# A feed-forward stage with block-scaled integers: normalization, copies and biases moved between the engines of one core, and its tile loop skewed

## The reference

```python
def _L2_ffn_ref(inputs, ln_w, ln_b, W1, b1, W2, b2):      # inputs = layernorm(x)
    bf16_round = lambda x: x.astype(bfloat16).astype(float32)
    def mx_quant(x):          # blocks of 32 along the last axis share one exponent
        s = x.shape
        xb = x.reshape(s[:-1] + (s[-1] // 32, 32))
        amax = max(abs(xb), axis=-1)
        scale = exp2(floor(log2(amax)) - 6)
        return clip(round(xb / scale), -128, 127) * scale
    def mx_linear(x, W, b):
        return bf16_round(mx_quant(x) @ mx_quant(W).T + b)
    x = residual = bf16_round(inputs)
    h = bf16_round(layernorm(x) * ln_w + ln_b)            # 256 wide
    h = mx_linear(h, W1, b1)                              # 1024 wide
    h = bf16_round(gelu_tanh(h))
    h = mx_linear(h, W2, b2)                              # 256 wide
    return bf16_round(residual + h)
...
x = x + tanh(g_ffn[2]) * _L2_ffn_ref(layernorm(x), ...)
```

## Time and profile before

| | |
|---|---|
| median of three runs | 966.0 us (963.3, 966.0, 970.25) |
| the profiled execution | 954.89 us, its span 953.1 us |
| TensorE busy over the span | 625.7 us, 66% |
| VectorE, ScalarE, GpSimd busy | 693.3, 318.1, 155.0 us |
| mean granted TensorE clock | 0.814 of full speed |
| stage 5 | 713.79 to 813.30 us of the span |

### The profile page before, as it was taken

One profiled execution on the slowest core, in us unless ns is written; L12 is line 12 of the kernel. 1 busy time (PEld: TensorE's weight loads), 2 busy tenths in 40 slices (PEclk: granted clock), 3 DMA queues, 4 the chain that ended last, 5 costly groups with the idle time before them and its releaser, 6 DMA issues. The chain is left out here.

```text
span 953.1 us, 9406 instructions
## 1 busy us (share of the span) xinstructions
PE 625.7 (66%) x2822; PEld 398.8 (42%) x2825; DVE 693.3 (73%) x1419; ACT 318.1 (33%) x543; POOL 155.0 (16%) x158
## 2 busy tenths in 40 slices
PE   5408998999973432389928488988970454339970
PEld 3303554555543431256817355555450222326540
DVE  5996699979969573597586759798859887843433
ACT  4004436545412321123234164655620322313210
POOL 0000001211200000344242001100114122014315
PEclk9759999999987655599968689999995565559995
DMA  8400002553558023134420032433527100013314
GB/s 238 101 13 0 7 0 45 88 89 66 89 127 244 0 61 136 39 108 125 101 61 17 1 88 53 96 77 86 133 45 175 46 1 1 22 37 94 93 60 128
DMA packets 57952, 71.17 MB, mean 75 GB/s; under 512 B 14920, under 2 KB 41424, under 8 KB 56752
## 3 DMA queue, kind: packets, MB, share of 16 engines
q1 hardware_dynamic: 45072, 42.53, 15.6%
q0 software_dynamic: 12832, 28.06, 14.9%
HBM read 43.43 MB, written 10.35 MB: 56 GB/s over the span
## 5 line engine op out<-in xcount | busy, mean ns | idle before, releaser
L521 PE MATMUL ps<-hT,regA 128*128 128x512 f32 x256 | 115.3, 593 | 1.3 <-ACT hT L437 1.3
L1855 PE MATMUL ps<-regA,regD 128*34 128x256 f32 x256 | 69.6, 395 | 16.3 <-DVE h L1973 10.8
L521 PEld LDWEIGHTS ps<-hT,regA 128*128 128x128 f32 x256 | 48.4, 190 | 52.1 <-issue 46.5
L532 PE MATMUL ps<-regA,regC 128*128 128x256 f32 x256 | 62.7, 388 | 6.8 <-DVE regC L651 5.3
L692 POOL DMA_DIRECT2D yssm<-regB x19 | 22.9, 1204 | 245.5 <-DVE regB L644 240.6
L532 PEld LDWEIGHTS ps<-regA,regC 128*128 128x128 f32 x256 | 46.7, 190 | 31.6 <-DVE regC L651 21.2
L447 ACT ACTIVATE regC<-ps 128x512 f32<-128x512 f32 x32 | 19.1, 597 | 91.1 <-PE ps L521 86.4
L1711 ACT ACTIVATE regA<-ps 128x512 f32<-128x512 f32 x64 | 38.1, 596 | 30.8 <-PE ps L1841 29.9
L636 DVE TENSOR_TENSOR_SCAN regB<-regB 128x512 f32<-128x512 f32 x38 | 44.5, 1212 | 2.8
L1242 POOL DMA_INDIRECT regA<-h_rows,regA x31 | 29.5, 952 | 73.6 <-DVE regA L1490 43.1
L1953 DVE TENSOR_REDUCE regC<-ps 128x4 f32<-128x960 f32 x64 | 39.7, 683 | 1.6 <-PE ps L1808 1.6
(11 more groups left out here) (400 smaller groups left out, 1524.9 us busy)
## 6 DMA issues: line engine op xcount, KB each, us to landing
yssm<-regB POOLq DMA_DIRECT2D x19, 512.0 KB, 5.0
regC<-bc_rows SPq DMA_DIRECT2D x26, 256.0 KB, 3.8
yssm<-regC POOLq DMA_DIRECT2D x13, 512.0 KB, 6.9
regB<-in_L_w SPq DMA_DIRECT2D x4, 1088.0 KB, 11.7
y_rows<-regA SPq DMA_DIRECT2D x31, 128.0 KB, 2.4
y_rows<-regB SPq DMA_DIRECT2D x23, 128.0 KB, 1.7
regB<-in_L_w SPq DMA_DIRECT2D x1, 2176.0 KB, 12.9
regC<-in_L_W SPq DMA_DIRECT2D x2, 1024.0 KB, 10.5
```

The costliest lines, as they stand in the source:

```text
L521: m = nc.tensor.matmul(ps[:, 2 + 2 * (u % 2) + j, :], w[:, k * 2048 + c * P:k * 2048 + (c + 1) * P], hT[:, k, hf * HALF:(hf + 1) * HALF], ...
L532: m = nc.tensor.matmul(ps[:, t // 2, (t % 2) * D:(t % 2 + 1) * D], itm[:, u % 2, t * P:(t + 1) * P], WDv[:, c // 2, c % 2, :], start=(c == ...
L1855: m = nc.tensor.matmul(ps[0:VW, 6 + j % 2, (n % 2) * S:(n % 2 + 1) * S], vaug[:, 2 * b + kt, hd, :], prob[:, n % 4, kt * S:(kt + 1) * S], ...
```

## The change

All of it is in stage 5.

- ScalarE does both normalizations, tile by tile, as `activation(Identity, scale=, bias=)`; VectorE computes scale and bias with one small operation more, and takes the statistics of `rb` tile by tile.
- The two bias rows are no more added by VectorE. They are loaded into partitions 0, 32 and 64 (`BROWS`) of `brows`, whose first 96 partitions (`NB5`) GpSimd clears before; ScalarE and GpSimd split them into three bfloat16 parts (`bcut`, `bsplit`), and TensorE adds them with one matmul more (`ones` times `bsplit`) in each bank of `up` and in the down product.
- The affine work (lnw, lnb) of pairs 0 and 2 goes to VectorE, that of pairs 1 and 3 stays on GpSimd.
- ScalarE copies the hidden tile out of PSUM (`hidden`) and the output tile (`output`); `result` on VectorE has two operations left.
- The loop is skewed: VectorE does raise(i), limit(i-1), result(i-3); ScalarE does hidden(i+1), gelu(i), the turned copy of i-2, output(i-3). TensorE's order is unchanged.

```diff
                 def _(sp):
-                    for dst, nm in ((lnw, "L2_lnw"), (lnb, "L2_lnb"), (b1, "L2_b1"), (b2, "L2_b2")):
+                    sp.wait_ge(s_bz, 1)
+                    for r in BROWS:
+                        sp.dma_start(brows[r:r + 1, 0:FF], a["L2_b1"].partition_broadcast(1)).then_inc(s_br, 16)
+                        sp.dma_start(brows[r:r + 1, FF:FF + D], a["L2_b2"].partition_broadcast(1)).then_inc(s_br, 16)
+                    for dst, nm in ((lnw, "L2_lnw"), (lnb, "L2_lnb")):
                         sp.dma_start(dst, a[nm].partition_broadcast(P)).then_inc(s_b, 16)
                     load_w7(sp)
 
                 def _(pool):
-                    pool.wait_ge(s_b, 64)
-                    for i in range(NT // 2):
-                        affine(i)
+                    nc.gpsimd.memset(brows[0:NB5, :], 0.0).then_inc(s_bz, 1)
+                    nc.gpsimd.memset(bsplit[0:NB5, :], 0.0).then_inc(s_bz, 1)
+                    for i in range(len(BROWS) - 1):
+                        pool.wait_ge(s_bcut, i + 1)
+                        nc.gpsimd.tensor_tensor(brows[0:NB5, :], brows[0:NB5, :], bcut[0:NB5, :],
+                                                ALU.subtract).then_inc(s_brest, 1)
+                    pool.wait_ge(s_b, 32)
+                    for n, i in enumerate((1, 3)):
+                        ...
 
                 def _(act):
+                    def normalize(dst, src, s_bias, s_done):
+                        act.wait_ge(s_bias, 1)
+                        for t in range(NT):
+                            nc.scalar.activation(dst[:, t, :], src[:, t, :], ACT.Identity, scale=lnsd[:, 0, t:t + 1],
+                                                 bias=lnsd[:, 1, t:t + 1]).then_inc(s_done, 1)
+                    def split_biases(i):
+                        if i == 0:
+                            act.wait_ge(s_br, 96)
+                            act.wait_ge(s_bz, 2)
+                        else:
+                            act.wait_ge(s_brest, i)
+                        r = BROWS[i]
+                        if i + 1 < len(BROWS):
+                            nc.scalar.copy(bcut[0:NB5, :], brows[0:NB5, :]).then_inc(s_bcut, 1)
+                            act.wait_ge(s_bcut, i + 1)
+                            nc.scalar.copy(bsplit[r:r + 1, :], bcut[r:r + 1, :]).then_inc(s_bsplit, 1)
+                        else:
+                            nc.scalar.copy(bsplit[r:r + 1, :], brows[r:r + 1, :]).then_inc(s_bsplit, 1)
                     norm_on_scalar(act, s_var, s_sd)
+                    normalize(rb, x, s_nb, s_rb)
+                    split_biases(0)
                     act.wait_ge(s_var2, 1)
                     nc.scalar.activation(lnsd[:, 1, :], lnsd[:, 0, :], ACT.Sqrt).then_inc(s_sd2, 1)
+                    normalize(h, rb, s_nb2, s_h2)
+                    split_biases(1)
+                    split_biases(2)
+                    def hidden(t):
+                        act.wait_ge(s_y1, t + 1)
+                        ...
+                        nc.scalar.copy(y1[:, t % 2, :], ps[:, 2 * (t % 2):2 * (t % 2) + 2, :]...).then_inc(s_y1b, 1)
+                    turned_input(0)
+                    turned_input(1)
+                    hidden(0)
+                    hidden(1)
+                    gelu(0)
+                    turned_input(2)
+                    turned_input(3)
+                    for i in range(1, NT + 3):
+                        if i + 1 < NT:
+                            hidden(i + 1)
+                        if i < NT:
+                            gelu(i)
+                        if 0 <= i - 2 < NT:
+                            turned_hidden(i - 2)
+                        if i >= 3:
+                            output(i - 3)
 
                 def _(pe):
+                    def add_bias(dst, c0, n):
+                        return nc.tensor.matmul(dst, ones[0:NB5, :], bsplit[0:NB5, c0:c0 + n], start=False, stop=True)
                     def up(t):
                         pe.wait_ge(s_q1T, t // 2 + 1)
                         if t >= 2:
                             pe.wait_ge(s_y1b, t - 1)
+                        if t == 0:
+                            pe.wait_ge(s_bsplit, len(BROWS))
                         for n in range(2):
                             ...
+                            m = add_bias(o_, n * HALF, HALF)
                         m.then_inc(s_y1, 1)
 
                 def _(dve):
+                    for i in range(NT + 3):
+                        if i < NT:
+                            if i >= 2:
+                                dve.wait_ge(s_q2, i - 1)
+                            raise_hidden(i)
+                        if 1 <= i <= NT:
+                            limit_hidden(i - 1)
+                        if i >= 3:
+                            result(i - 3)
```

More of the change, by code:

```diff
@@ L2093, in _ @@
                         nc.scalar.copy(q1T[:, :, i * 2 * P:(i + 1) * 2 * P], turned(4 + i, psb)).then_inc(s_q1T, 1)
[L2094 to L2105, removed]
+                    def hidden(t):
+                        act.wait_ge(s_y1, t + 1)
+                        if t >= 2:
+                            act.wait_ge(s_g1, t - 1)
+                        nc.scalar.copy(y1[:, t % 2, :], ps[:, 2 * (t % 2):2 * (t % 2) + 2, :].rearrange("p b n -> p (b n)")
+                                       ).then_inc(s_y1b, 1)
@@ new lines, in output @@
+                    def output(t):
+                        act.wait_ge(s_y2, t + 1)
+                        if t >= 2:
+                            act.wait_ge(s_x, t - 1)
+                        nc.scalar.copy(y2[:, t % 2, :], ps[:, 6 + t % 2, 0:D]).then_inc(s_y2b, 1)
+                    turned_input(0)
[5 more added lines that the diff above has]
+                    turned_input(3)
@@ L2148, in _, with statistics @@
                     v = Steps(dve, s_v)
[L2149 to L2152, removed]
-                    for i in range(NT // 2):
-                        dve.wait_ge(s_hb, i + 1)
+                    def statistics(src, s_src, s_var_, s_sd_, s_bias):
+                        for t in range(NT):
+                            if s_src is not None:
+                                dve.wait_ge(s_src, t + 1)
+                            v.mark(nc.vector.bn_stats(lnst[:, t, :], src[:, t, :]))
+                        v.settle()
+                        for t in range(NT):
+                            v.mark(nc.vector.bn_aggr(lnmv[:, t, :], lnst[:, t, :]))
+                        v.settle()
+                        nc.vector.tensor_scalar(lnsd[:, 0, :], lnmv[:, :, 1], LN_EPS, None, ALU.add).then_inc(s_var_, 1)
+                        dve.wait_ge(s_sd_, 1)
+                        v.link(nc.vector.reciprocal(lnsd[:, 0, :], lnsd[:, 1, :]))
+                        nc.vector.scalar_tensor_tensor(lnsd[:, 1, :], lnmv[:, :, 0], -1.0, lnsd[:, 0, :], ALU.mult,
+                                                       ALU.mult).then_inc(s_bias, 1)
@@ new lines, in _ @@
+                    statistics(x, None, s_var, s_sd, s_nb)
+                    statistics(rb, s_rb, s_var2, s_sd2, s_nb2)
+                    q1v, tmpv = (w.rearrange("p (i n) -> p i n", n=2 * D) for w in (q1, tmp))
+                    for i in range(NT // 2):
+                        if i % 2 == 0:
+                            if i == 0:
+                                dve.wait_ge(s_b, 32)
+                            dve.wait_ge(s_h2, 2 * i + 2)
+                            v.link(nc.vector.tensor_tensor(pair_of(h, i), pair_of(h, i), row(lnw), ALU.mult))
+                            v.link(nc.vector.tensor_tensor(hbv[:, i].rearrange("p (t n) -> p t n", n=D), pair_of(h, i), row(lnb),
+                                                           ALU.add))
+                        else:
+                            dve.wait_ge(s_hb, i // 2 + 1)
@@ L2155, in _ @@
                         mx_scales(v, blocks(hbv[:, i]), am[:, i])
                         mx_round(v, blocks(hbv[:, i]), blocks(q1v[:, i]), blocks(tmpv[:, i]), am[:, i], s_q1)
[L2157 to L2174, removed]
```

72 lines of the change are left out of this document (43 added, 29 removed).

## The result

The changed kernel takes 981.46 us (median of 4 runs, 976.45 to 986.73) where the kernel before takes 965.0 beside it (963.3 to 970.25): ratio 1.0162, 95% interval 1.0094 to 1.023. It is slower, by 0.9 to 2.3%. The profiled execution of after took 980.05 us, with a span of 978.2.

What follows compares the result with a forecast made beforehand. VectorE was taken to bound stage 5 before, a serial chain across engines after; lead-in +1.4, turns +12.1, tail -4.8 and 0.8 for semaphores gave +9.5 on 966.0, so 975.5 us, range 964 to 985.

Steps and rivals of the forecast that it cites:

- The serial loop: Stage 5's tile loop: limit to next limit becomes one chain across engines, 9.82 us a tile against 7.34; 62%, 971 to 981.
- The signs named for it: Loop: raises 9.3 to 9.8 apart, released by gelu; hidden waits for the bias matmul; limit no longer waits for GpSimd.
- One sign against it: End of stage 5's lead-in: the prediction is wrong if the first limit falls outside 754 to 761.
- The turns: Five turns from first to sixth limit in stage 5: 47.6 us against 35.51, so +12.1.
- the clock: TensorE in the five turns: one up in five taken at 2.4 GHz, 1.5 us less over the five.
- never fast: Bound for the five turns with no up at 2.4 GHz: 5 x 9.82 = 49.1 us.
- The lead-in: Stage 5's start to first limit: limit(0) at about 757.9 against 756.50, +1.4 us, bounds -2 and +4.
- The tail: Sixth limit to the end of stage 5: 16.5 us against 21.29, so -4.8.
- the rival of 985: Loop: GpSimd's subtraction takes the shared port before limit, adding 1.91 us in each of five turns; 985 us, chance 9%.
- the allowance of 0.8 for semaphore steps: Added to the +8.7 us sum for semaphore steps such sums leave out, giving +9.5.

Runs made afterwards that it cites:

- e1: Changed kernel with ScalarE's gelu(i) put ahead of hidden(i+1), same work; stage 5 took 91.20 us against 111.36 in the changed kernel.
- e2: Changed kernel with ScalarE's order gelu, turned copy, hidden, output; stage 5 89.08 us, time ratio 0.9866 to the kernel before.
- e4: Changed kernel without the bias matmuls in up and down, the splitting kept; stage 5 took 105.29 us, its five turns 45.19.
- e8: Changed kernel with both normalizations put back on VectorE; stage 5 took 112.98 us against 111.36 in the changed kernel.
- e3: e2 with the subtraction of the rounding constant moved from GpSimd to VectorE, ahead of limit; stage 5 89.08 us, ratio 0.9927 to the kernel before.
- e7: e3 with GpSimd splitting the bias rows during the first normalization, ScalarE copying only three single rows afterwards; stage 5 85.32 us, ratio 0.9854 to the kernel before.
- e0: The kernel before, unchanged, profiled once more; stage 5 took 99.50 us against 99.51 in its first profile.

## Why the prediction was right

**Direction and mechanism.** Slower by over 1% had the largest chance, 47%, against 43% for within 1%, so the direction was forecast by a narrow margin; the measured interval, from 0.9%, just takes in less than 1% too. The serial loop had 62%, with 971 to 981; the measured 981.46 is at the upper end of that. The chain limit, transposes, up, hidden, gelu, raise was put at 9.82 us a turn; measured 9.89 in four of five turns. e1 and e2 show it by its order, e4 by one link's length. The signs named for it came: raises 9.6 to 9.9 apart, released by the gelu; hidden waiting for the bias matmul; no wait of limit for GpSimd. One sign against it seems to be there, the first limit at 770.00 instead of 754 to 761, but the stage began 11.28 later in this execution: counted from its start the limit came at 44.93, which is 758.7 in the prediction's times.

**The turns, +12.1 forecast, +13.6 measured.** The term mis-sized is the clock: one burst of up in five was taken at 2.4 GHz, worth 1.5. One turn of five was indeed shorter, 9.56, but by 0.33, since only a part of its up ran at 2.4 GHz. The granted clock in the turns was 0.57 (0.69 in the earlier trace rows). e8, with the same loop and no fast up, has 49.46, so the sum of the links for "never fast", 49.1, is 0.4 short; that 49.13 equals it is chance.

**The lead-in, +1.4 forecast, +2.2 measured.** ScalarE's eight normalizing operations took 4.04 (0.50 a tile, as taken). The estimate from the Trainium skill ("ScalarE: Activation LUTs", "What ACT_TABLE_LOAD costs"), 0.49, agrees. The scale and bias were ready 12.2 us after the stage's start, forecast 12.3, though it was the small operation behind the reciprocal that was blocked. The 0.8 that is missing lies in GpSimd: its subtraction took 2.60, not 2.2, and its first affine operation of pair 1 took 1.71 instead of 1.3, held behind VectorE's last limit of pair 0. That limit was blocked itself (3.10), which the sum left out; it cost VectorE nothing more, as it had to wait 2.49 for pair 1 anyway. From the last quantizing limit to the first limit of the loop the sum was right to 0.1.

**The tail, -4.8 forecast, -4.0 measured.** From the sixth to the seventh limit it took 6.48, where the prediction gave 4.8 to 6.7 and took 5: GpSimd did take the port ahead of result, whose first operation took 2.00. From the seventh limit to the end it was 10.8 for 11.1.

**Limit and GpSimd.** In after limit takes its 1.22, being 0.16 ahead (770.00 against 770.16 in the first turn), and GpSimd's operation is stretched instead, 2.82 to 2.83 for 1.91: the rival of 985 did not come. With the rule of the Trainium skill that whoever starts first has the port ("SBUF — State Buffer", "SBUF: two separate sides") the trace agrees.

**The sum.** +9.5 forecast against +11.85 for the stage; the three misses above add to 3.1, all three to the slow side, and the allowance of 0.8 for semaphore steps covered part of it. The median came 6.0 above the forecast; 2.4 of that is the stage, and the rest can't be told from the scatter outside it. That it stayed in the range, up to 985, owes something to luck: the upper end was set by the rival of 985, which did not come.

## What to carry to other kernels

Before skewing a loop, write down each engine's new order and follow one tile through it: a wait placed ahead of independent work on an in-order engine can turn engines that overlapped into one chain, and here two swapped calls were worth 20 us. Then lighten the engine that is busiest; here, without the order, it bought nothing. Work given to GpSimd beside a VectorE full of two-input operations isn't free: give it what runs while VectorE reduces, reads PSUM or idles.

## What the runs showed of the hardware

- When GpSimd waited for the port behind limit, it got it ahead of VectorE's next operation: result's first operation took 2.00 in every full turn of after and e2, where GpSimd subtracts, and 0.28 in e3, where it does not. Back-to-back issue didn't keep the port for VectorE. In two turns of e1, where result came later, it took 0.29 and 0.78.
- Even operations of 16 elements a partition were held for a whole GpSimd operation (1.24 for 0.17 in e7), while a block maximum over 512 elements kept its 0.69 beside GpSimd (748.21 in after, under an operation of GpSimd from 748.14 to 749.41).
- Nearly the same busy share of TensorE went with different granted clocks in the five turns: 0.57 in after (27.86 of 49.13, two bursts a turn), 0.69 in before (19.68 of 35.51, one burst a turn). The same code also got 0.69 in one execution and 0.73 in another (before, e0). No run shows the cause.
